# First sequence's feed-forward and first queries of the second layer tile by tile, and two loads placed later

## What is computed

```python
# layer 0, end: feed-forward with fake quantisation, per token row
h   = layernorm(x) * g1 + b1
q   = clip(round(h * 127/max|h|), -128, 127)            # one scale per row
u   = gelu(q @ W1q.T * scale + w1b)                      # width 1024
u   = layernorm(u) * g2 + b2
q2  = clip(round(u * 127/max|u|), -128, 127)
x   = x + q2 @ W2q.T * scale2 + w2b
# layer 1, start: attention of x over the context with one head of width 256
qe  = layernorm(x) @ Wq.T + bq
s   = (qe @ (ctx @ Wk.T + bk).T) / 16 + mask             # 256 x 4096 scores a sequence
x   = x + softmax(s) @ ctx @ Wv.T + bv
```

## Time and profile before

| | us |
|---|---|
| median of 3 runs | 976.12 |
| lowest and highest run | 973.57, 976.53 |
| the profiled execution | 976.69 |
| its span | 974.6 |
| PE, DVE, ACT, POOL busy in the span | 896.3, 608.5, 479.8, 105.7 |
| mean granted TensorE clock | 0.968 |

### The profile page before, as it was taken

How to read it: one execution, slowest core, us unless ns; L and a number is a source line. 1 busy time by engine, 2 the same in 40 slices (tenths; PEclk the granted TensorE clock), 3 DMA queues, 4 the chain that set the end, 5 groups by cost and what they waited for, 6 DMA issues and landing times.

```text
span 974.6 us, 15294 instructions
## 1 busy us (share of the span) xinstructions
PE 896.3 (92%) x5988; PEld 529.3 (54%) x5988; DVE 608.5 (62%) x1083; ACT 479.8 (49%) x953; POOL 105.7 (11%) x118
## 2 busy tenths in 40 slices
PE   6888999999999999999998898689899999989878
PEld 3445544444555555545544686444784874555635
DVE  5778688778874548888833586847424227379442
ACT  3331557777765557777788432324321210576211
POOL 3320011111000000000000200101000006245100
PEclk9999999999999999999999999869899999999979
DMA  9775634354222011222432600604545640000000
GB/s 312 259 202 199 204 104 141 114 162 138 86 67 76 33 59 56 74 74 74 168 123 79 242 1 1 239 21 152 194 173 208 224 145 29 1 1 1 1 1 22
DMA packets 68836, 108.68 MB, mean 112 GB/s; under 512 B 7062, under 2 KB 42902, under 8 KB 66838
## 3 DMA queue, kind: packets, MB, share of 16 engines
q1 hardware_dynamic: 67100, 101.40, 31.5%
q10 hardware_dynamic: 1664, 6.29, 1.8%
HBM read 93.77 MB, written 13.89 MB: 110 GB/s over the span
## 4 chain that ended last, share of the span: by engine, by line
PE 78%; DVE 6%; ACT 6%; issue 3%; DMA 3%; SPq 2%; POOL 0%; ACTq 0%; DVEq 0%
PE psum L1833 13%; PE psum L1815 11%; PE psum L1786 9%; PE psum L2207 6%; PE psum L2180 5%; PE psum L1969 5%; PE psum L1763 4%; PE psum L2300 4%; PE psum L1753 4%; PE psum L1982 3%; ACT arena L756 3%; DMA kparts<-arena 2%; PE psum L2354 2%; PE psum L2339 1%; PE psum L2372 1%
## 5 line engine op out<-in xcount | busy, mean ns | idle before, releaser
L1119 DVE TENSOR_REDUCE arena<-psum 128x1 f32<-128x1024 f32 x256 | 301.3, 1218 | 109.9 <-PE psum L1786 109.4
L756 ACT ACTIVATE arena<-psum 128x512 f32<-128x512 f32 x512 | 264.6, 603 | 62.1 <-PE psum L1815 61.0
L1815 PE MATMUL psum<-arena 99*128 99x256 bf16 x1024 | 160.2, 274 | 8.9 <-ACT arena L756 4.8
L1786 PE MATMUL psum<-arena 96*128 96x512 bf16 x512 | 152.9, 381 | 8.9 <-DVE arena L1119 4.0
L1815 PEld LDWEIGHTS psum<-arena 99*128 99x128 bf16 x1024 | 79.4, 97 | 107.1 <-ACT arena L756 50.3
L1833 PE MATMUL psum<-arena 128*32 128x256 f32 x2048 | 136.8, 385 | 0.0
L1833 PEld LDWEIGHTS psum<-arena 128*32 128x32 f32 x2048 | 53.5, 109 | 75.4 <-ACT arena L756 36.9
L1753 PE MATMUL psum<-arena 128*128 128x512 f32 x128 | 62.9, 619 | 8.4 <-DMA arena<-ctxT 8.4
L1763 PE MATMUL psum<-arena 128*128 128x256 f32 x256 | 64.7, 389 | 2.1 <-issue 2.1
L1786 PEld LDWEIGHTS psum<-arena 96*128 96x128 bf16 x512 | 49.0, 98 | 28.5 <-DVE arena L1119 11.9
L649 POOL TENSOR_TENSOR arena<-arena 128x512 bf16<-128x512 f32 x34 | 41.4, 1218 | 194.3 <-DVE arena L1105 191.7
(11 more groups left out here) (244 smaller groups left out, 959.1 us busy)
## 6 DMA issues: line engine op xcount, KB each, us to landing
arena<-kparts SPq DMA_DIRECT2D x192, 128.0 KB, 2.9
kparts<-arena SPq DMA_DIRECT2D x32, 384.0 KB, 3.6
arena<-ctxT SPq DMA_DIRECT2D x20, 512.0 KB, 4.9
arena<-ctx SPq DMA_DIRECT2D x2, 4096.0 KB, 15.1
arena<-mask SPq DMA_DIRECT2D x8, 1024.0 KB, 5.3
arena<-mask ACTq DMA_DIRECT2D x4, 1024.0 KB, 14.5
arena<-ctxT SPq DMA_DIRECT2D x1, 4096.0 KB, 13.9
arena<-ctxT SPq DMA_DIRECT2D x4, 1024.0 KB, 8.2
```

Source lines behind the costliest of these rows:

```text
L756: nc.scalar.activation(PR[step % 4][:, pair * CH:(pair + 1) * CH], ring_bank(slot), ACT.Exp)\
L1119: nc.vector.tensor_reduce(MX[g % 2][:, col:col + 1], unit_banks(n).rearrange("p b n -> p (b n)"), AX.X, ALU.max).then_inc(s_maxed, 1)
L1786: last = nc.tensor.matmul(out, q, KST[g % 2][0:ROWS, j, at], start=True, stop=not masked, skip_group_check=True)
L1815: last = nc.tensor.matmul(ring_heads(slot)[:, u, :], KST[gg % 2][0:KROWS, j, kc * P:(kc + 1) * P], QST[0:KROWS, G * g + j, b * S:(b + 1) * S],
```

## The change

On tiles 0 and 1 the pair operations become operations of one tile each, and the lists of PE, DVE and ACT are put in another order. Nine inverse square roots of this stage, which were ACT's root and DVE's reciprocal, become one power of -0.5 on GpSimd each. GpSimd's multiplication by g2 and ACT's centring stay for tile 3 alone; tile 1 goes as tile 0 did. On SP, masks 0 and 1 and then the context wait for the first `d_turned2` (the first `turn_hidden` behind the join).

```diff
 # SyncE
-            sp.wait_ge(on["c_fuse"], 2 * IT)
-            load(CTXK[0], ..., "ctxk_loaded0")
             sp.wait_ge(on["c_out"], 4)
+            sp.wait_ge(on["d_turned2"], 1)
...
-            for n in range(5):
+            load_mask(0)
+            load_mask(1)
+            load(CTXK[0], ..., "ctxk_loaded0")
+            for n in range(2, 5):
                 load_mask(n)
 # GpSimd
+            nc.gpsimd.memset(NHALF, -0.5).then_inc(built, 1)
...
-            for b in range(B):
-                pool.wait_ge(on["d_centred"], b + 1)
-                odd = UH[2 * b + 1][:, 0, :]
-                nc.gpsimd.tensor_tensor(odd, odd, row("g2"), ALU.mult)...
+            def power(first, last):
+                powers[0] += 1
+                pool.wait_ge(ln_var, powers[0])
+                part = SD[:, 4 + first:4 + last]
+                nc.gpsimd.tensor_tensor(part, part, NHALF[:, first:last], ALU.pow).then_inc(ln_sd, 1)
+            power(0, 1)
+            power(1, 2)
+            power(0, 1)
+            power(1, 2)
+            power(0, 1)
+            power(2, 4)
+            power(1, 2)
+            power(2, 4)
+            pool.wait_ge(on["d_centred"], 1)
+            odd = UH[3][:, 0, :]
+            nc.gpsimd.tensor_tensor(odd, odd, row("g2"), ALU.mult)...
+            power(2, 4)
 # ScalarE
-            root(0, 2)
             copy_hb(1)
+            nc.scalar.activation(TABLES[:, 0:1], ONES[:, 0:1], ACT.Gelu)
...
-            copy_quantised(0)
-            gelus(0)
-            root(0, 2)
-            centre_odd(0)
+            copy_quantised_tile(0)
+            gelus(0, 2)
+            copy_quantised_tile(1)
+            gelus(2, 4)
             copy_hidden(0)
+            copy_turned_tile(0)
+            copy_queries_tile(0)
+            copy_folded_tile(0)
             copy_hidden(1)
-            root(2, 4)
-            root(0, 2)
-            copy_turned_half(0)
-            copy_queries(0)
-            copy_folded(0)
+            copy_turned_tile(1)
+            copy_queries_tile(1)
+            copy_folded_tile(1)
             copy_quantised(1)
-            gelus(1)
             key_exps(0)
-            root(2, 4)
-            centre_odd(1)
+            gelus(4, 8)
             copy_exps(0, 0)
             copy_exps(0, 2)
+            centre_odd(3)
             key_exps(1)
...
 # VectorE (add_mixed, add_down now end with ask_root;
 # centre_for_keys begins with take_power)
+            add_mixed(0, 1, TT)
+            add_mixed(1, 2, TT + 1)
+            for i in range(2):
+                take_power()
+                normalise_for_up(i)
+            hidden(0, 0)
+            hidden(0, 1)
+            gate(1, 0)
+            gate(1, 1)
+            hidden_stats(0, 0)
+            hidden_stats(0, 1)
+            aggregate(2, 0, 1)
+            ask_root(0, 1)
+            gate(1, 2)
+            hidden(0, 2)
+            hidden(0, 3)
+            gain(0)
+            gate(1, 3)
+            take_power()
+            shift(0)
+            find_scale(0)
+            quantise_hidden(0)
+            hidden_stats(0, 2)
+            hidden_stats(0, 3)
+            aggregate(2, 1, 2)
+            ask_root(1, 2)
+            add_down_bias(0, 1)
+            gain(1)
+            take_power()
+            done()
+            add_down(0, 1, TT + 2)
+            shift(1)
             centre_for_keys(0)
+            find_scale(1)
+            quantise_hidden(1)
+            add_mixed(2, 4, TT + 3)
 # between mask units of tile 0: add_down(1), centre_for_keys(1),
 # normalise_for_up(2) behind unit 2, normalise_for_up(3) behind unit 5;
 # of tile 1: hidden(1, n-1) behind units 1 to 4, hidden_stats behind 5 to 7
...
             bias_exps(1)
-            find_scale(2)
             copy_exps(0, 1)
-            quantise_hidden(2)
+            hidden_stats(1, 3)
+            aggregate(2, 2, 4)
+            ask_root(2, 4)
             copy_exps(0, 3)
+            take_power()
+            turn_mean(3)
+            gain(2)
+            shift(2)
+            copy_exps(0, 5)
+            find_scale(2)
+            quantise_hidden(2)
+            copy_exps(0, 7)
...
 # TensorE, end of mix()
+                turn_quantised(0, 0)
                 fuse(1, 0)
-                fuse(1, 1)
-                turn_quantised(0)
-                fuse(1, 2)
...
-                for n in range(4):
-                    project_up(0, n)
+                project_up(0, 0)
+                project_up(0, 1)
+                fuse(1, 1)
+                turn_quantised(0, 1)
+                fuse(1, 2)
+                project_up(0, 2)
+                project_up(0, 3)
                 fuse(1, 3)
                 project_out(1)
 # TensorE, behind the join
-            for i in range(2):
-                turn_hidden(i)
-                project_down(i)
+            turn_hidden(0)
+            project_down(0)
-            turn_half(HLE, 0, 2 * TT)
+            turn_tile(HLE, 0, 2 * TT)
             turned()
-            project_queries(0)
-            fold_queries(0)
-            bias_queries(0)
-            turn_quantised(1)
+            queries_tile(0)
+            fold_tile(0)
+            turn_hidden(1)
+            pe.wait_ge(on["e_qc_copied"], 1)
+            key_scores(0, 0)
+            bias_tile(0)
+            project_down(1)
+            key_scores(0, 1)
+            key_scores(0, 2)
+            key_scores(0, 3)
+            turn_tile(HLE, 1, 2 * TT)
+            key_scores(0, 4)
+            turned()
+            queries_tile(1)
+            key_scores(0, 5)
+            pe.wait_ge(on["e_cq_copied"], 1)
+            fold_tile(1)
+            key_scores(0, 6)
+            bias_tile(1)
+            key_scores(0, 7)
+            turn_quantised(1, 0, 1)
+            pe.wait_ge(on["e_qc_copied"], 2)
             for n in range(8):
                 key_scores(1, n)
+                if n < 4:
+                    project_up(1, n)
             for n in range(4):
                 turn_exps(0, n)
             weigh_context(0, 0)
-            turn_hidden(2)
             turn_exps(0, 4)
             turn_exps(0, 5)
             weigh_context(0, 1)
+            turn_hidden(2)
             turn_exps(0, 6)
             turn_exps(0, 7)
-            project_down(2)
             weigh_context(0, 2)
+            project_down(2)
...
```

More of the change, by code:

```diff
@@ L1271, in aggregate, with take_power, add_to_x @@
                 done()
-            def add_to_x(name, n, add, first=0, last=TT):
+            def take_power():
+                roots[0] += 1
+                dve.wait_ge(ln_sd, roots[0])
+            def add_to_x(name, n, add, first=0, last=TT, ahead=None):
+                ahead = TT * n + first if ahead is None else ahead
                 for i in range(first, last + 1):
@@ L1318, in gate, with add_mixed @@
                                                op0=ALU.add, op1=ALU.mult).then_inc(on["c_gated"], 1)
-            def add_mixed(b):
+            def add_mixed(first, last, ahead):
                 add_to_x("c_out", 1, lambda i: nc.vector.tensor_tensor(
-                    X[:, i, :], X[:, i, :], psum[:, OUT_BANKS[i], 0:256], ALU.add), 2 * b, 2 * b + 2)
+                    X[:, i, :], X[:, i, :], psum[:, OUT_BANKS[i], 0:256], ALU.add), first, last, ahead)
+                ask_root(first, last, 1.0 + 1e-5, 1e-5 * 1e-5)
             for b in range(B):
@@ L1357, in quantise_scale, with normalise_for_up @@
                 done()
[L1359 to L1364, removed]
+            def normalise_for_up(i):
+                part = HLQ[:, i % 2, :]
+                mark(nc.vector.scalar_tensor_tensor(out=part, in0=X[:, i, :], scalar=MV[:, 2 * i:2 * i + 1], in1=row("g1"),
+                                                    op0=ALU.subtract, op1=ALU.mult))
@@ L1365, in normalise_for_up @@
                 done()
[L1366 to L1369, removed]
+                mark(nc.vector.scalar_tensor_tensor(out=part, in0=part, scalar=SD[:, 4 + i:5 + i], in1=row("b1"),
+                                                    op0=ALU.mult, op1=ALU.add))
@@ L1433, in quantise_hidden, with add_down @@
                 nc.vector.tensor_scalar(QH[i], QH[i], -128.0, None, ALU.max).then_inc(on["d_quant2"], 1)
-            def add_down(b):
+            def add_down(first, last, ahead):
                 add_to_x("d_down", 2, lambda i: nc.vector.scalar_tensor_tensor(
                     out=X[:, i, :], in0=psum[:, DOWN_BANKS[i], 0:256], scalar=OSC[:, i:i + 1], in1=X[:, i, :],
-                    op0=ALU.mult, op1=ALU.add), 2 * b, 2 * b + 2)
-            def centre_for_keys(b):
-                for i in (2 * b, 2 * b + 1):
+                    op0=ALU.mult, op1=ALU.add), first, last, ahead)
+                ask_root(first, last)
@@ L1442, in centre_for_keys, with copy_cq @@
+            def centre_for_keys(*tiles):
+                take_power()
+                for i in tiles:
                     centred(HLE, X, i).then_inc(h_ready, 1)
-            def copy_cq(b):
```

(24 more changed lines are left out.)

248 lines of the change are left out of this document (117 added, 131 removed).

## The result

The changed kernel takes 959.12 us (957.55 to 962.59 in 4 runs) against 975.52: a ratio of 0.9839, interval 0.9808 to 0.9871, so 12.6 to 18.7 us faster. The forecast was 11.7 us off the 976.12 known then, to 964.4, in a range of 960.0 to 970.5. The profiled execution took 957.55 us, its span 955.8.

A forecast was written before the change was run, and what follows sets the result against it. PE was taken as the bound, held by DVE's order of work and then a PE-ACT chain at the slow clock; 8.2 + 5.7 - 2.1 = 11.8 us off 976.69, stated as 964.4, range 960 to 970.5.

The forecast's parts named there:

- Tile 0 quantised: Normalising and quantising tile 0 alone on DVE: done at 622.6 in place of 627.03, about 4.4 us earlier.
- the arms' end: PE's last matmuls of the arms: delayed by about 0.3 us, to 621.2, as `gate(1, 3)` comes behind `gain(0)`.
- First key scores: Tile 0's chain up to the key scores, partly at the low clock: start at 635.8, 14.1 us earlier.
- The sixteen units: Key-score loops with tile 1's chain moved in: 33.6 us plus 1.6 for the clock, end at 671.0, 8.2 us earlier.
- 3.2 us of the units at half speed, 1.6 more: Start of the key-score units: full clock back only near 639, costing 1.6 us (between 0 and 3).
- Turning and weighing: Behind the units, with the awaited DVE copy moved up: 6.75 us in place of 12.5, 5.7 won.
- 2.1 lost: PE's wait at `turn_hidden(2)`: tile 2 quantised 13.2 us behind the units, PE there at 11.1.
- The powers: Nine GpSimd powers at 0.3 us each, costing nothing; up to 0.7 us free under DVE's other work.
- Rival D: Slow GpSimd powers hold tile 0's first, its centring and tile 2: 969.7 at 3 us each, 970.9 at 3.41; chance 9%.
- The loads: Masks asked for at 623.2, landing 5.2 us later, context 15.1 behind them: both there before needed.
- C: Instruction fetch at the join behind the arms, no longer covered by a wait: 4.8 us on top, 969.2; chance 12%.
- E: A later PE instruction page queues behind SP's six megabytes of loads: up to 18 us, 982, slower; chance 4%.

The follow-up runs named there:

- both tiles ahead: Changed kernel with tile 1's down projection, sum, centring, turning and queries put back ahead of the first key scores: 965.95 us, ratio 0.9883 to the kernel before.
- third look at the kernel before: The kernel before, unedited, profiled once more: median 969.12 us, stage 129.40 us.
- shift late: Changed kernel with `shift(2)` moved behind the third odd copy on DVE: 963.16 us, ratio 0.986 to the kernel before.

## Why the prediction was wrong in size

The forecast lies 5.3 us above the median (964.4 against 959.12), 0.6 of it because the kernel before came out at 975.52 and not 976.12. The profiled pair shows two shares beyond the forecast: 2.6 us in the stage (14.4 won, 11.8 forecast) and 2.7 us behind it, which the forecast put at nothing. Step by step in the stage, each measured time with 1.7 us added for the earlier start of this execution:

- **Tile 0 quantised** at 622.6: 620.7 + 1.7 = 622.4. Right, and so was the arms' end.
- **First key scores** at 635.8: 634.3 + 1.7 = 636.0. Right, the clock's fall included. Undoing it (both tiles ahead) confirms the mechanism.
- **The sixteen units** until 671.0: 667.6 + 1.7 = 669.3. The step that failed here is "3.2 us of the units at half speed, 1.6 more". I took the time of the clock's return from the one case in the kernel before; it came 3.3 us earlier and the term was 0. The third look at the kernel before, where it came back about 6 us earlier behind the same work, shows that one case couldn't give it.
- **Turning and weighing**, 6.75 us: 6.6. Right. `turn_hidden(2)` "2.1 lost": 1.09. The failed step is that `shift(2)` "runs beside GpSimd's product" and is the one held. It began 0.12 us ahead of it and took 1.28 us, not 2.65, and the product was held. So tile 2 was quantised 12.1 us behind the units in place of 13.2, with PE there at 11.1 as forecast.
- **The powers** at 0.3 us: 0.55 to 0.76, once 1.52, for 0.52 us of DVE's time. Rival D had the right place and a price too high.
- **The loads**, whose new place has no term in the sum, because the packet "ran at once even beside the context's traffic": worth 2.5 us in this order. The forecast of the kernel as changed doesn't suffer, as the join was covered to 1.29 us in it. But the argument against C was wrong: the packet did run at once, in 0.93 us, and PE waited all the same. What the Trainium skill says of taken branches, that the engine may have to wait for a DMA fetch of its target (Runtime: NRT & Kernel Launch, "Instruction fetch mechanics"), fits these runs as far as that: 2.83 us beside traffic, at most 1.29 without. Also wrong is E's "the same queue": the packet is on q8 of the profile and the context on q1.

Of the 2.6 us missing in the stage, 1.7 lie at the end of the units (9.9 us earlier in place of 8.2) and 0.9 behind the first weighing (1.2 lost in place of 2.1).

**Behind the stage** lies the largest single miss, a term put at nothing. "Behind them it has the same work as before, so what is won by then should stay won" held for the work and not for its speed: 242.84 us in place of 245.57, 1.7 of it at the sixteen matmuls and 1.1 at the router. Why the clock spares them after the change stays open, and no row of the trace before could have told it.

The profiled pair's spans differ by 18.8 us: 14.4, 2.7 and the 1.7 us earlier start, which the change didn't make. The third look at the kernel before shows how far one execution may mislead. My range took bounds for the operations and none for the clock in untouched stages.

## What to carry to other kernels

When a stage is bound by a chain over several engines, start the next stage's long matmul loop on the first tile that is ready and put the other tile's chain between its units: that was half of the stage's gain here. No run takes back the tile-by-tile quantising by itself; that the wait behind the arms fell from 6.26 to 1.29 us by it is read from the rows. Keep a copy that TensorE waits for ahead of long work on the same engine, and take such work out of the loop before it. Moving a load away from a branch's join was worth 2.5 us here, 1.5 of it waiting, and nothing while another wait covered the join. And give a forecast of small terms a bound of 2 or 3 us for the clock in stages that keep their instructions.

## What the runs showed of the hardware

- The same sixteen matmuls took 3.72 us at the full clock and 5.3 to 5.4 us where the low level fell on them; edits of the changed kernel in an earlier stage switched between the two.
- The clock's return isn't fixed by the work in front of it: behind the same instructions and waits of one kernel it came 52 us into the stage twice and 46 us once.
- A wait of 2.41 us in the midst of work was followed by the low clock (shift late), one of 1.09 us at the same place wasn't.
- GpSimd's product of 1024 columns takes 2.37 us alone and 3.4 us when a DVE operation with two operands had just begun; a power of one column takes 0.55 to 0.76 us, and 1.52 us in that case.
- Behind a taken branch TensorE stood still for 2.83 us beside a load at 370 GB/s, and for 1.29 us at most without it, though the instruction packet took no longer (0.93 and 1.25 us).
